# Graph network layers on one core: gate weights split sooner, the last sum in another order, its last half product by quarters, the last tile stored by halves

## The reference

```python
u = _rgcn(x, edge_index, edge_type, weight, root, bias)      # 625 x 1024
z = concat([u, x], axis=1) @ w_gate + b_gate                 # w_gate is 2048 x 1024
h = tanh(u) * z + x * (1.0 - z)
x = _layernorm(x + h)
```

## Time and profile before

| | us |
|---|---|
| median of 3 runs | 887.26 |
| lowest, highest | 886.17, 887.57 |
| the profiled execution | 886.36 |
| its span, first to last instruction | 884.5 |
| mean granted TensorE clock | 0.979 |
| TensorE busy | 833.7 |
| VectorE busy | 675.1 |
| ScalarE busy | 447.4 |

### The profile page before, as it was taken

The page is one execution under the profiler, slowest core; times in us unless marked ns, Lnnn a source line. Parts: engine busy times, 40 slices in busy tenths (PEclk is TensorE's granted clock), DMA queues, the critical chain, the costliest instruction groups (busy, mean ns, idle before and its releaser), DMA issues.

```text
span 884.5 us, 16323 instructions
## 1 busy us (share of the span) xinstructions
PE 833.7 (94%) x6332; PEld 591.4 (67%) x6332; DVE 675.1 (76%) x975; ACT 447.4 (51%) x633; POOL 16.9 (2%) x38
## 2 busy tenths in 40 slices
PE   4569999999989999999999999999999999999996
PEld 2435574545876786776876866867867768769452
DVE  7985579599877777778778778677777787777777
ACT  4874555556455525534445355355255344445721
POOL 1000000000000000000000000000000000000000
PEclk9669999999999999999999999999999999999999
DMA  9110035120222022022021120220220220311302
GB/s 292 38 54 0 0 131 205 72 96 1 96 96 96 1 96 96 2 95 76 19 95 34 60 95 1 94 95 0 95 95 0 95 82 14 119 40 57 119 24 92
DMA packets 30326, 63.42 MB, mean 72 GB/s; under 512 B 981, under 2 KB 4689, under 8 KB 30289
## 3 DMA queue, kind: packets, MB, share of 16 engines
q1 hardware_dynamic: 29977, 62.64, 20.1%
q10 hardware_dynamic: 312, 0.26, 0.1%
HBM read 57.71 MB, written 5.18 MB: 71 GB/s over the span
## 4 chain that ended last, share of the span: by engine, by line
PE 77%; DVE 15%; ACT 4%; issue 3%; DVEq 0%; POOL 0%; ACTq 0%; POOLq 0%
PE psP L1084 44%; PE psA L1154 20%; PE psP L931 5%; PE psA L920 3%; DVE wsplit L1329 2%; DVE wsplit L1323 2%; PE psP L1009 1%; PE psA L876 1%; PE psP L888 1%; DVE p_mem L1367 1%; DVE wsplit L1458 1%; DVE stats L1533 1%; DVE cu_mem L1577 1%; DVE p_mem L1366 1%; DVE xT L1295 1%
## 5 line engine op out<-in xcount | busy, mean ns | idle before, releaser
L1084 PE MATMUL psP<-wsplit,xT 128*128 128x256 f16 x2592 | 296.4, 273 | 3.2 <-ACT vec L770 2.8
L1084 PEld LDWEIGHTS psP<-wsplit,xT 128*128 128x128 f16 x2592 | 254.3, 98 | 37.5 <-issue 3.1
L1154 PE MATMUL psA<-p_mem,cu_mem 128*128 128x512 f16 x800 | 175.3, 379 | 0.0
L1084 PE MATMUL psP<-wsplit,x 128*128 128x256 f16 x1296 | 150.3, 273 | 1.7 <-DVE key_mem L1643 1.5
L1154 PEld LDWEIGHTS psA<-p_mem,cu_mem 128*128 (+1 forms) x800 | 78.3, 98 | 90.9
L1084 PEld LDWEIGHTS psP<-wsplit,x 128*128 128x128 f16 x1296 | 126.7, 98 | 16.8 <-issue 2.2
L1329 DVE SCALAR_TENSOR_TENSOR wsplit<-stage,sc,wsplit 128x1024 f16<-128x1024 f32 x90 | 114.8, 1279 | 27.2 <-ACT wsplit L614 27.2
L614 ACT ACTIVATE wsplit<-stage,sc 128x1024 f16<-128x1024 f32 x90 | 100.6, 1137 | 15.0 <-DVE sc L1231 9.1
L1608 DVE SCALAR_TENSOR_TENSOR cu_mem<-psA,coef,cu_mem 128x512 f32<-128x512 f32 x80 | 60.1, 751 | 33.0 <-PE psA L1154 30.9
L614 ACT ACTIVATE wsplit<-x,sc 128x1024 f16<-128x1024 f32 x54 | 61.7, 1143 | 39.2 <-PE psP L1084 32.6
L1329 DVE SCALAR_TENSOR_TENSOR wsplit<-x,sc,wsplit 128x1024 f16<-128x1024 f32 x54 | 69.2, 1282 | 10.3 <-ACT wsplit L614 10.2
(11 more groups left out here) (189 smaller groups left out, 802.0 us busy)
## 6 DMA issues: line engine op xcount, KB each, us to landing
stage<-in_L_gnn_weight SPq DMA_DIRECT2D x16, 2048.0 KB, 7.8
stage<-in_L_gnn_w_gate SPq DMA_DIRECT2D x4, 2048.0 KB, 7.8
x_home<-x SPq DMA_DIRECT2D x5, 512.0 KB, 2.6
x<-x_home SPq DMA_DIRECT2D x5, 512.0 KB, 5.5
stage<-in_L_gnn_W_rel SPq DMA_DIRECT2D x4, 572.0 KB, 10.7
x<-in_x SPq DMA_DIRECT2D x4, 512.0 KB, 5.3
xT<-in_L_gnn_root SPq DMA_DIRECT2D x1, 2048.0 KB, 8.1
stage<-in_L_gnn_root SPq DMA_DIRECT2D x1, 2048.0 KB, 9.4
```

What stands on the lines that cost most here:

```text
L1084: last = nc.tensor.matmul(psP[:, bank, (col + tt) * FB:(col + tt + 1) * FB], lhs[tt](a, c), split_block(n, b)[:, c, :], start=(first and t ...
L1154: last = nc.tensor.matmul(psA[:, (NT * h + t) % 2, :], cnt8[:, r, s, t * P:(t + 1) * P], p_part[h][a][:, s, :], start=(s == 0 and a == 0), ...
```

## The change

- `raw_high` and `raw_low` take a list of blocks. Blocks 0 and 1 of `U_GU` are split on ScalarE behind the second scaled tile, ahead of the turned tile 0, and on VectorE behind the low halves of tile 0; blocks 2 and 3 stay where all four were. The two bias additions of `gate_21` are now at the head of `gate_12`.
- The last sum: ahead of the product of a tile, VectorE makes the base 2x + zx * d for both halves, with d = tanh(u) - x (`z_base`), and ScalarE then multiplies d by `cz` in place (`u_scaled`). Behind each product come `tt` (PSUM times scaled d) and `tt` (plus base). Reciprocal and shift of the tile before (`out_row`) stand behind `z_base`. ScalarE waits for both columns of `cz` before its loop over the tiles.
- The last half product (tile 4, right half) is made as two quarters (`raw_quarter`, 24 matmuls of 256 columns each) in two banks; VectorE adds each and takes its statistics by itself, and those of the left half by quarters too (`stats_end`, four groups).
- VectorE normalizes the last tile in two halves. SyncE stores rows 0 to 111 of each half when it is ready, ScalarE row 112: four transfers where two were.

```diff
@@ -399,6 +404,7 @@
             for k in range(k0, k1):
                 batch(k, k % 2)
 
+        LAST = [(1, 0, (2 * NT - 1) % NT), (1, 1, 2 * NT % NT)]
         GATE = [(0, 0), (1, 0), (0, 1), (1, 1)] + [(t, h) for t in range(2, NT) for h in range(2)]
 
         def gate_turn(n):
@@ -422,6 +428,11 @@
             for a, v in arrays:
                 engine.dma_start(edges[ROWS16:EP - 1, a, :], span(v, ROWS16, EP - 1)).then_inc(loaded, 16)
                 engine.dma_start(edges[EP - 1:EP, a, 0:RUN], v[EDGES - RUN:EDGES].unsqueeze(0)).then_inc(loaded, 16)
+
+        def store_end(engine, r0, r1, h):
+
+            r, cols = (NT - 1) * P, slice(h * HALF, (h + 1) * HALF)
+            engine.dma_start(out_d[r + r0:r + r1, cols], x[r0:r1, NT - 1, cols]).then_inc(out_stored, 16)
 
         @block.sync
         def _(sp):
@@ -487,10 +498,10 @@
             for t in range(NT - 1):
                 sp.wait_ge(out_ready, t + 1)
                 sp.dma_start(out_d[t * P:(t + 1) * P, :], x[:, t, :]).then_inc(out_stored, 16)
-            sp.wait_ge(last_ready, 1)
-            for r0, r1 in ((0, EVEN), (EVEN, TAIL)):
-                sp.dma_start(out_d[(NT - 1) * P + r0:(NT - 1) * P + r1, :], x[r0:r1, NT - 1, :]).then_inc(out_stored, 16)
-            sp.wait_ge(out_stored, 16 * (NT + 1))
+            for h in range(2):
+                sp.wait_ge(last_ready, h + 1)
+                store_end(sp, 0, EVEN, h)
+            sp.wait_ge(out_stored, 16 * (NT + 3))
 
 
         @block.gpsimd
@@ -593,10 +604,11 @@
                     nc.scalar.activation(land, st[:, part], ACT.Abs,
                                          accum_out=am[:, slot, n:n + 1]).then_inc(wsum_ready, 1)
 
-            def raw_high(i, slot):
+            def raw_high(i, slot, blocks=range(4)):
 
                 act.wait_ge(scale_step, 4 * i + 4)
-                for n, (k, f) in enumerate(RAW):
+                for n in blocks:
+                    k, f = RAW[n]
                     b = weight_blocks(i) + n
                     if i >= U_GU:
                         act.wait_ge(prod, STEPS * (SEVEN - 1) + b % RING_W + 1)
@@ -820,9 +832,11 @@
             act.wait_ge(row_scaled, 1)
             for t in range(NT):
                 nc.scalar.activation(us[:, t, :], u[:, t, :], ACT.Copy, scale=rows_f[:, 1, 2, t:t + 1]).then_inc(us_ready, 1)
+                if t == 1:
+                    raw_high(U_GU, 0, (0, 1))
                 if t == 1 or t == 3:
                     split_hi(2, t // 2, uT, 1.0)
-            raw_high(U_GU, 0)
+            raw_high(U_GU, 0, (2, 3))
             weight_sum(U_GU + 1, 1, slot_load(U_GU + 1))
 
             def u_tanh(t):
@@ -834,14 +848,22 @@
             raw_high(U_GU + 1, 1)
             for t in range(3, NT):
                 u_tanh(t)
+            act.wait_ge(cz_ready, 2)
             for t in range(NT):
                 if t + 2 < NT:
                     split_hi(2, t + 2, uT, 1.0)
+                for h in range(2):
+                    act.wait_ge(base_ready, 2 * t + h + 1)
+                    uv = u[:, t, h * HALF:(h + 1) * HALF]
+                    nc.scalar.activation(uv, uv, ACT.Copy, scale=cz[:, h, t:t + 1]).then_inc(u_scaled, 1)
                 if t:
                     act.wait_ge(out_factors, 2 * t)
                     nc.scalar.activation(x[:, t - 1, :], x[:, t - 1, :], ACT.Identity, bias=shift[:, t - 1:t],
                                          scale=rstd[:, 2, t - 1:t]).then_inc(out_ready, 1)
                 ln_deviation(1, t)
+            for h in range(2):
+                act.wait_ge(last_ready, h + 1)
+                store_end(act, EVEN, TAIL, h)
 
 
         @block.tensor
@@ -929,6 +951,16 @@
                     s, cols = s0 + 2 * (c // KB), slice(c % KB * FB, (c % KB + 1) * FB)
                     for a, b, first in ((0, 0, c == 0), (0, 1, False), (1, 0, False)):
                         last = nc.tensor.matmul(out, lhs[:, a, c, bass.ts(t, P)], wsplit[:, s:s + 2, b, cols],
+                                                start=first, stop=(c == DC - 1 and a == 1))
+                return last
+
+            def raw_quarter(out, lhs, i, t, f):
+
+                s0 = weight_blocks(i) % RING_W + f
+                for c in range(DC):
+                    for a, b, first in ((0, 0, c == 0), (0, 1, False), (1, 0, False)):
+                        last = nc.tensor.matmul(out, lhs[:, a, c, bass.ts(t, P)],
+                                                split_block(s0 + 2 * (c // KB), b)[:, c % KB, :],
                                                 start=first, stop=(c == DC - 1 and a == 1))
                 return last
 
@@ -1208,7 +1240,11 @@
                 if t + 1 < NT:
                     turn(2, t + 1, us, us_ready)
                 gate_product(2 * t)
-                gate_product(2 * t + 1)
+                if t + 1 < NT:
+                    gate_product(2 * t + 1)
+            for f in range(2):
+                pe.wait_ge(z_done, 1 + gate_turn(NT - 1 + f))
+                raw_quarter(psP[:, (2 * NT - 1 + f) % NT, 0:FB], uT, U_GU + 1, NT - 1, f).then_inc(z_full, 1)
 
 
         @block.vector
@@ -1315,9 +1351,10 @@
                 dve.wait_ge(wo_hi, 1)
                 stt(lo, st, sc_f[:, scale_col(U_WO, 1), 2:3], hi, ALU.mult, ALU.subtract).then_inc(wo_lo, 1)
 
-            def raw_low(i, slot):
-
-                for n, (k, f) in enumerate(RAW):
+            def raw_low(i, slot, blocks=range(4)):
+
+                for n in blocks:
+                    k, f = RAW[n]
                     b = weight_blocks(i) + n
                     dve.wait_ge(whi_ready, b + 1)
                     stt(split_block(b % RING_W, 1), raw_block(i, slot, k, f), sc_f[:, scale_col(i, slot), 2:3],
@@ -1539,10 +1576,6 @@
                 dve.wait_ge(ln_std[k], t + 1)
                 dve.wait_ge(ln_var[k], t + 1)
                 return nc.vector.reciprocal(rstd[:, 1 + k, t:t + 1], std[:, 1 + k, t:t + 1])
-
-            def norm_apply(k, t, ready):
-                step(norm_reciprocal(k, t))
-                ts(x[:, t, :], x[:, t, :], mv[:, k, t, 0:1], rstd[:, 1 + k, t:t + 1], ALU.subtract, ALU.mult).then_inc(ready, 1)
 
 
             for t in range(NT):
@@ -1744,13 +1777,14 @@
                 left, right = zx[h][:, 2:4, 0:FB], zx[h][:, 2:4, FB:HALF]
                 dve.wait_ge(prod, STEPS * j + 6)
                 stt(left, bank(3), f, left, ALU.mult, ALU.add).then_inc(c21_ready, 1)
+
+            def gate_12(h):
+                j, f = 2 * R1 + h, gate_f[:, h:h + 1]
+                left, right = zx[h][:, 2:4, 0:FB], zx[h][:, 2:4, FB:HALF]
                 dve.wait_ge(c22_ready, j + 1)
                 tt(right, right, bias_of(h, 1), ALU.add)
                 dve.wait_ge(c21_ready, j + 1)
                 tt(left, left, bias_of(h, 0), ALU.add)
-
-            def gate_12(h):
-                j, f = 2 * R1 + h, gate_f[:, h:h + 1]
                 right = zx[h][:, 0:2, FB:HALF]
                 dve.wait_ge(prod, STEPS * (j + 1))
                 dve.wait_ge(p16_ready, j + 1)
@@ -1794,40 +1828,68 @@
             row_scales([rows[:, 1, a, :] for a in range(4)], rowmax[:, 1, :].bitcast(I32), row_scaled)
             gate_11(1)
             split_lo(2, 0, uT, 1.0)
+            raw_low(U_GU, 0, (0, 1))
             gate_22(1)
             split_lo(2, 1, uT, 1.0)
             gate_21(1)
-            raw_low(U_GU, 0)
+            raw_low(U_GU, 0, (2, 3))
             gate_12(1)
-            step(ts(cz[:, 0, :], rows_f[:, 1, 3, :], sc_f[:, scale_col(REL, 0), 3:4], None, ALU.mult))
+            ts(cz[:, 0, :], rows_f[:, 1, 3, :], sc_f[:, scale_col(REL, 0), 3:4], None, ALU.mult).then_inc(cz_ready, 1)
             unit_scale(U_GU + 1, 1)
             raw_low(U_GU + 1, 1)
             dve.wait_ge(scale_step, 4 * UNITS)
-            step(ts(cz[:, 1, :], rows_f[:, 1, 3, :], sc_f[:, scale_col(REL, 1), 3:4], None, ALU.mult))
+            ts(cz[:, 1, :], rows_f[:, 1, 3, :], sc_f[:, scale_col(REL, 1), 3:4], None, ALU.mult).then_inc(cz_ready, 1)
+
+            def z_base(t):
+
+                for h in range(2):
+                    cols = slice(h * HALF, (h + 1) * HALF)
+                    step(tt(zx[h][:, t, :], zx[h][:, t, :], u[:, t, cols], ALU.mult))
+                    stt(zx[h][:, t, :], x[:, t, cols], 2.0, zx[h][:, t, :], ALU.mult, ALU.add).then_inc(base_ready, 1)
+
+            def out_row(t):
+                norm_reciprocal(1, t).then_inc(out_factors, 1)
+                dve.wait_ge(out_factors, 2 * t + 1)
+                ts(shift[:, t:t + 1], mv[:, 1, t, 0:1], rstd[:, 2, t:t + 1], -1.0, ALU.mult, ALU.mult).then_inc(out_factors, 1)
 
             dve.wait_ge(x1_back, 16 * NT)
             for t in range(NT):
                 if t + 2 < NT:
                     split_lo(2, t + 2, uT, 1.0)
                 dve.wait_ge(tanh_ready, t + 1)
-                step(tt(u[:, t, :], u[:, t, :], x[:, t, :], ALU.subtract))
-                for h in range(2):
-                    n = 2 * t + h
```

(47 more changed lines are left out.)

## The result

The changed kernel takes 891.32 us (median of 6 runs, 890.32 to 891.88), the kernel before 887.31 (6 runs, 886.17 to 887.95): ratio 1.0047, 95% interval 1.0036 to 1.0058, 4.0 us slower. The prediction said 891.0, 887.8 to 893.5.

What follows compares the result with a forecast made beforehand. VectorE, without slack, was taken as the bound of the last stretch. Terms -1.2 + 3.3 + 2.6 - 0.6 = +4.1 us gave 890.5 from the profiled 886.36, 891.3 from the median 887.26; forecast 891, range 887.8 to 893.5.

Steps and rivals of the forecast that it cites:

- The bound: Last stretch: VectorE has no slack, never idle from 855.53 to 876.45; what TensorE gains does not move the end.
- (a): Kernel end: TensorE sets it, so the change does what it promises, 4.2 us less, 883; 5 in 100.
- start of VectorE's loop: VectorE's loop over the tiles: earlier splits bring 2.13 us, waiting for cz costs 0.17; 833.25 becomes 831.3.
- start of tile 2: After tiles 0 and 1 on VectorE: waits swallow their extra work, start moves from 855.53 to 854.3, 1.2 us sooner.
- tiles 2 and 3: VectorE's tiles without cover: extra operation and wait for ScalarE cost 1.65 us each, 3.3 us together.
- tile 4: Last tile on VectorE: 1.7 us like the others, quarters 0.18 + 0.6, half normalizations 0.1; together 2.6 us more.
- stores: Last tile's stores: half the bytes leave 0.4 us earlier, second issue carries half; 0.6 us off, bounds 0 and 1.
- Inside the tile: VectorE's tile: PSUM multiplication 0.75 us, ScalarE's scaling 0.63; 7.59 becomes 9.3 us, 1.65 to 1.7 more.
- (b): End stays within 0.2% (1.8 us) as waits swallow more; no VectorE wait for ScalarE counted as -1.2; 8 in 100.
- The quarters: Last tile on VectorE: more statistics and sum operations, 256 wide, cost 0.18 + 0.6 us more.
- (c): ScalarE becomes the link: scaling queues behind its 1.24 us application, last three tiles wait 1.2 longer each, 894.8; 4 in 100.
- (d): Earlier splits delay the first turned tile by more than 0.1 us; about 0 at the end, no separate chance given.

Runs made afterwards that it cites:

- hoist_quarters: Kernel before plus earlier splits, four differences made in VectorE's waits, tile 4's right half with base ahead and product by quarters, stores by halves: 883.01 us.
- split_only: The kernel before with only the earlier weight splits and the two bias additions moved as in the change: 885.02 us, ratio 0.9979 to before.
- no_scaling: The changed kernel without ScalarE's scaling of the difference; the factor goes into VectorE's operation behind the product: 889.62 us.
- whole_last: The changed kernel with the last half product whole, its sum and statistics in one piece, stores by halves kept: 889.98 us.
- late_split: The changed kernel with all four weight blocks split where they were before: 892.92 us.

## Why the prediction was right, step by step

**The bound.** Right for the changed kernel: from the last turned tile on VectorE works without a pause but for ScalarE's scaling and square root, and `hoist_quarters` shows the opposite case that rival (a) described: there TensorE ends last, and there a shorter tail pays (the quarters clearly, the two operations by 0.5 us in the profile alone). One sentence of the reading was too wide: that what TensorE gains does not move the end. In the kernel before, the turned tile 4 is TensorE's, and `split_only` moved the end by 2.0. The sum didn't rest on that sentence, since it took the start of tile 2 from the chain. That chain is right as well: it gave VectorE 0.3 + 0.6 us of waiting before the turned tiles 3 and 4, behind ScalarE's square root, and the trace has 0.85 us at each, in place of 2.45 and 2.32.

**The terms**, counted from the first turned tile:

| term | predicted | measured |
|---|---|---|
| start of VectorE's loop | -1.95 | 24.00 - 25.91 = -1.91 |
| start of tile 2 (`split_lo` of tile 4) | -1.2 | 46.80 - 48.19 = -1.39 |
| tiles 2 and 3 | +3.3 | 9.27 + 9.22 - 7.62 - 7.59 = +3.28 |
| tile 4 | +2.6 | 11.70 - 9.05 = +2.65 |
| stores | -0.6 | 3.07 - 3.5 = -0.43 |
| sum | +4.1 | +4.11 |

Every term has its sign and nearly its size. That the sum agrees to 0.01 us is luck: the start of tile 2 and the stores missed by 0.19 and 0.17, in opposite directions.

**Inside the tile** two prices were off and nearly cancelled. The multiplication with a PSUM source took 0.69 us, not 0.75: the PSUM source alone does not cost the 0.06 us more of `L1819`. ScalarE's scaling took 0.72, not 0.63. `no_scaling` measured what the wait for ScalarE was worth, less the 0.06 us that the factor then costs VectorE: 1.24 us in tiles 2 to 4 (0.43, 0.43 and 0.38), where rival (b) had put 1.2 on three tiles, and 0.48 more because tile 2 starts sooner (46.32 us in place of 46.80).

**The quarters** cost 0.8 by `whole_last`, as the sum had it (0.18 + 0.6). The rule of the Trainium skill that bears on it (VectorE: DVE Perf Modes, section on the TRN2 errata: a fixed cost for each operation, so tiles of 512 elements or more) agrees with the runs: 128x256 took 0.42 us and 128x512 0.69, half the work for 61% of the time. The table of 58 cycles in the same section of the Trainium skill, from which the prediction took its lower figure, would give 0.33 and 0.59; the section says itself that this row under-predicts, and the formula that it states for an f32 `tensor_tensor` addition gives, as an estimate, 0.42 and 0.69, which the traces confirm.

**The stores** gave less than the 0.6 said, and with the half normalizations against them about 0.2 in the profiles and nothing that the times show. That the second queue would be worth at most its issue time (the Trainium skill, Trainium Kernel Development and Optimization, Key Constraints) agrees: ScalarE's two issues lay beside SyncE's two, 0.78 beside 0.80 us, and no gain beyond that can be seen.

**Rivals.** (a) 883: it would have needed VectorE at the last quarter by TensorE's end; it came to the first of the two 6.8 us late (882.45 against 875.69). (b) falls with the tile period of 9.2. (c) falls: `L861`, the application of the tile before, started behind the second scaling each time. (d) did not happen: ScalarE took up the first turned tile 0.64 us behind its start (809.47 - 808.83), before 0.63. But where the splits stand was put too lightly there, as a matter of TensorE's cover: `late_split` shows that the position of the splits is worth 1.6 to 2.2 us here, through ScalarE's and VectorE's queues and not through TensorE.

## What to carry to other kernels

Shortening what follows a product pays only where the product's engine ends last; where the consuming engine has no slack, work moved ahead of the product is still its work, and two operations behind plus two ahead are more than three. First look for the waits into which the work can go (here four differences of 1.2 us, two into each wait of some 2.4 us before a turned tile), and cut the tail afterwards: the same ideas that lost time in the changed kernel, now on the last half alone, took 1.7 us off once that was done (884.73 to 883.01). A helper engine in the middle of a serial chain costs its own duration plus two handovers in every round, even if it idles otherwise, less what the waiting engine can do meanwhile: here 0.72 us and 0.07 for the handovers in tile 0, where VectorE waits 0.79, and 0.46 in the later tiles, where it makes reciprocal and shift first.

## What the runs showed of the hardware

A `tensor_tensor` multiplication with one source in PSUM took 0.69 us for 128x512, the same as from SBUF, while `scalar_tensor_tensor` with a factor per partition and a PSUM source took 0.75. That points to the factor as what costs the 0.06 us; no run has the factor without PSUM at this width. ScalarE's copy with a scale per partition, SBUF to SBUF in f32 in place, took 0.72 us for 128x512, more than the 0.63 of a plain copy to f16. And the part of the kernel that no edit touched reached the first turned tile between 807.34 and 808.83 us in the profiles, by and large latest where the granted clock had fallen twice on the way. With effects of 1 us a profile should be counted from a point behind which the edits lie.
